# First experts' weights loaded during the first convolution, into a buffer shared with its centred input; ScalarE's copies of x in another order

## What is computed

```
x = x + _L0_conv_ref(_ln_c(x), ...)          # norm over channels, 7x7 depthwise convolution + bias
t = _to_tokens(x)                            # 9216 tokens of 128 channels
t = t + _L0_ffn_ref(_ln_t(t), Wg, W1, W2)    # 8 experts, each token goes to its best 2: silu(x@W1[e])@W2[e]
x = _from_tokens(t, x)
x = x + _L1_conv_ref(_ln_c(x), ...)          # upsample, leaky relu, clip, downsample
t = _to_tokens(x)
t = t + _L1_ffn_ref(_ln_t(t), ...)           # 8 gated experts, best 2
```

## Time and profile before

| | |
|---|---|
| time, median of 3 runs | 1369.09 us (1368.41 to 1370.15) |
| profiled execution, its own time | 1366.47 us |
| profiled execution, span | 1364.7 us |
| TensorE / VectorE / ScalarE / GpSimd busy | 80% / 68% / 47% / 54% of the span |
| first convolution | 0 to 154 us of the span |
| routing before the first block | 156 to 264 us |
| first layer's blocks | from 264 us |

### The profile page before, as it was taken

The page is one execution under the profiler, slowest core; times in us unless marked ns, Lnnn a source line. Parts: engine busy times, 40 slices in busy tenths (PEclk is TensorE's granted clock), DMA queues, the critical chain, the costliest instruction groups (busy, mean ns, idle before and its releaser), DMA issues. The chain is left out here.

```text
span 1364.7 us, 26463 instructions
## 1 busy us (share of the span) xinstructions
PE 1086.2 (80%) x6194; PEld 857.1 (63%) x6194; DVE 930.4 (68%) x3628; ACT 642.2 (47%) x1379; POOL 739.2 (54%) x719
## 2 busy tenths in 40 slices
PE   1499422499999998999389889789879679999982
PEld 0499412388887887989255555455545368888872
DVE  5766344388666675665366767667776588888897
ACT  1456334355555543444434745555654425555441
POOL 0233336567777777654440663663663776666652
PEclk9999855599999998999689989889989779999996
DMA  9243153322222224221610121121110223333498
GB/s 203 84 115 111 31 175 88 81 66 77 75 79 74 76 76 159 84 69 48 188 51 1 48 61 36 38 67 38 29 30 17 63 77 94 92 93 93 115 247 246
DMA packets 100984, 119.24 MB, mean 87 GB/s; under 512 B 29041, under 2 KB 81712, under 8 KB 99950
## 3 DMA queue, kind: packets, MB, share of 16 engines
q1 hardware_dynamic: 68031, 70.36, 20.1%
q0 software_dynamic: 20928, 40.15, 9.9%
q10 hardware_dynamic: 11887, 7.12, 1.9%
HBM read 67.55 MB, written 46.27 MB: 83 GB/s over the span
## 5 line engine op out<-in xcount | busy, mean ns | idle before, releaser
L637 POOL DMA_INDIRECT routed<-r_xn,r_slot x160 | 176.3, 1102 | 201.7 <-DVEq L626 158.7
L1170 POOL DMA_INDIRECT routed<-r_xn,r_slot x160 | 157.9, 987 | 80.4 <-issue 59.2
L1284 POOL DMA_INDIRECT answers<-c_x x152 | 150.8, 992 | 81.0 <-ACT c_x L1277 52.4
L1633 POOL DMA_INDIRECT answers<-c_c x152 | 146.6, 965 | 87.5 <-issue 65.0
L2058 PE MATMUL c_pz<-c_c,down 116*120 116x512 f32 (+1 forms) x392 | 193.3, 609 | 0.0
L1268 PE MATMUL r_ps_xy<-w,c_x 128*128 x1216 | 165.8, 280 | 22.9 <-DVE e_xl L1225 22.3
L1268 PEld LDWEIGHTS r_ps_xy<-w,c_x 128*128 128x128 f32 x1216 | 148.9, 193 | 32.2 <-issue 31.5
L1258 DVE COPY c_x<-r_ps_ht 128x512 f32<-128x512 f32 x152 | 104.3, 686 | 62.9 <-PE r_ps_ht L1250 61.1
L2032 PE MATMUL c_py<-c_xh,gl 121*116 121x512 f32 (+1 forms) x196 | 118.5, 604 | 30.1 <-DVE c_xl L2171 22.3
L1277 ACT ACTIVATE c_x<-r_ps_xy,c_x 128x128 f32<-128x128 f32 x152 | 55.7, 367 | 147.1 <-PE r_ps_xy L1268 145.4
L2181 DVE SCALAR_TENSOR_TENSOR c_c<-c_a 116x1024 f32<-116x1024 f32 (+1 forms) x60 | 76.9, 1281 | 67.6 <-ACT c_a L2119 66.5
(11 more groups left out here) (274 smaller groups left out, 2836.5 us busy)
## 6 DMA issues: line engine op xcount, KB each, us to landing
answers<-answers SPq DMA_DIRECT2D x23, 480.0 KB, 4.4
c_c<-routed SPq DMA_DIRECT2D x159, 66.0 KB
c_w<-in_w SPq DMA_DIRECT2D x26, 393.8 KB, 3.7
c_x<-routed SPq DMA_DIRECT2D x152, 66.0 KB
routed<-r_xn,r_slot POOLq DMA_INDIRECT x320, 2.4
c_x<-in_xh SPq DMA_DIRECT2D x4, 1170.0 KB, 8.5
w1l<-in_w SPq DMA_DIRECT2D x2, 2048.0 KB, 10.3
out<-x ACTq DMA_DIRECT2D x16, 240.0 KB
```

The costliest lines, as they stand in the source:

```text
L637: ro.nc.gpsimd.indirect_dma_start(ro.xs, bass.IndirectOffsetOnAxis(ap=ro.slot[0:px, q, c:c + 1], axis=0), ro.xn[0:px, q, k, t, :], None).t ...
L1170: ro.nc.gpsimd.indirect_dma_start(ro.xs, bass.IndirectOffsetOnAxis(ap=ro.slot[0:px, q, c:c + 1], axis=0), ro.xn[0:px, q, k, t, :], None).t ...
L1284: ex.nc.gpsimd.indirect_dma_start(ex.ys, bass.IndirectOffsetOnAxis(ap=ex.dest[:, slot:slot + 1], axis=0), ex.y[:, slot, :], None).then_inc ...
L1633: ex.nc.gpsimd.indirect_dma_start(ex.ys, bass.IndirectOffsetOnAxis(ap=ex.dest[:, s:s + 1], axis=0), ex.y[:, s, :], None).then_inc(ex.store ...
```

## The change

1. `cen` and the first layer's W1 and W2 now share one buffer (`c0_cen_w`, 26 x 384 floats a partition). For that `cen` is laid out with the channel outermost. Each quarter of it that `centre` writes now steps 384 floats (1536 bytes) from element to element, ScalarE's `square` reads it with the same step, and GpSimd reads a run.
2. The weights are loaded in four halves of 1 MB by SyncE in the convolution's channel loop, after the ring loads 10, 14, 20 and 25, each behind a wait until `normed` tells that the channels in its place have been used. At the end of the phase SyncE waits for all four (`w_loaded`). The two weight DMAs of the second phase are gone, and with them ScalarE's wait for them.
3. The shared buffer's last columns serve as three of the eight landing slots.
4. ScalarE's copies of x after group 4 now come as `COPIED` says: 5, 6 | 7, 8 | 9, 10 | 11 | 12, 13 beside groups 1 to 5, and 14 to 19 one a step in the first six block steps. `first_half` of group 0 comes before normalise of group 1, and the third root of variances one group later. VectorE's measures of groups 7 and 8, and the scale of that batch, come one group later too.

```diff
-        cen = sb("c0_cen", [P, NW, CIN])
+        cen = wt.shared[:].rearrange("p (c n) -> p n c", n=NW)
...
                 sp.dma_start(wring[0:CP, i % WRING, :], io["w0"][i]).then_inc(w_in[i % WRING], 16)
+                if i in WEIGHT_STEPS:
+                    weights_load_half(wt, sp, io, normed, WEIGHT_STEPS.index(i), w_loaded)
             sp.wait_ge(route_consts, 16 * 9)
             sp.wait_ge(blank_in, 16)
+            sp.wait_ge(w_loaded, 16 * len(WEIGHT_STEPS))
...
+WEIGHT_STEPS = (10, 14, 20, CIN - 1)
...
+def weights_load_half(wt, sp, io, normed, n, w_loaded):
+
+    layer_two, half = divmod(n, 2)
+    dst, name = (wt.w2, "w2_0") if layer_two else (wt.w1f, "w1_0")
+    cols = EXPERTS * FF // 2
+    covered = (n + 1) * cols
+    sp.wait_ge(normed, min(-(-covered // NW), CIN))
+    some = slice(half * EXPERTS // 2, (half + 1) * EXPERTS // 2)
+    src = io[name][:, some].rearrange("p e c d -> p (e c d)") if layer_two else io[name][:, some].rearrange("p e f -> p (e f)")
+    sp.dma_start(dst[:, half * cols:(half + 1) * cols], src).then_inc(w_loaded, 16)
...
+        COPIED = (range(0), range(5, 7), range(7, 9), range(9, 11), range(11, 12), range(12, 14), range(14, 14))
...
             for g in MOVED_BY_SP:
                 first_move(ro, sp, c0_x, g)
-                if g == MOVED_BY_SP[3]:
-                    weights_load(wt, sp, io, 0, w_in)
...
             def high_w(e):
-                act.wait_ge(w_in, 32)
...
                 for k in range(3):
-                    if g == (0, 1, 3)[k]:
+                    if g == (0, 1, 4)[k]:
                         first_root(ro, act, k)
+                if g == 1:
+                    first_half(ro, act, 0)
                 first_normalise(ro, act, g)
-                if g:
+                if g > 1:
                     first_half(ro, act, g - 1)
...
-                if 0 < g < BEFORE:
-                    for n in range(3 * g + 2, 3 * g + 5):
-                        first_copy_x(ro, act, n)
+                for n in COPIED[g]:
+                    first_copy_x(ro, act, n)
...
+                if s < GROUPS - COPIED[BEFORE].stop:
+                    first_copy_x(ro, act, COPIED[BEFORE].stop + s)
...
-                if g < 2:
-                    for n in range(BATCHES[2][0] + 2 * g, BATCHES[2][0] + 2 * g + 2):
+                if g in (0, 2):
+                    for n in range(BATCHES[2][0] + g, BATCHES[2][0] + g + 2):
                         first_measure(ro, dve, n)
                         first_spread(ro, dve, n)
-                    if g == 1:
+                    if g == 2:
                         first_variance(ro, dve, 2)
-                elif g == 2:
+                elif g == 3:
                     first_scale(ro, dve, ch, 2)
-                elif g == 3:
                     for n in range(4):
                         table(0, 1 + n)
```

More of the change, by code:

```diff
@@ L148, in after, with conv0_phase @@
         need(self.eng, self.sem, self.base + self.n, beat)
-def conv0_phase(nc, io, r, xs, x):
+def conv0_phase(nc, io, r, xs, x, wt, w_loaded):
     with ExitStack() as ctx:
@@ L386, in __init__, with take_high @@
         self.down = sb("down", [P, N_DOWN * TPX])
+WEIGHT_STEPS = (10, 14, 20, CIN - 1)
+class SharedWeights:
+    def __init__(self, nc, ctx):
+        self.shared = ctx.enter_context(nc.sbuf_tensor("c0_cen_w", [P, NW * CIN], F32))
+        cut = lambda n: self.shared[:, n * EXPERTS * FF:(n + 1) * EXPERTS * FF]
+        self.w1f, self.w2, self.rest = cut(0), cut(1), self.shared[:, 2 * EXPERTS * FF:]
+        self.w1l = self.w1f.bitcast(F32R)
+    def take_high(self, nc, ctx):
+        self.w1h = ctx.enter_context(nc.sbuf_tensor("w1h_0", [P, EXPERTS * FF], F32R))
+def weights_load_half(wt, sp, io, normed, n, w_loaded):
[7 more added lines that the diff above has]
+    sp.dma_start(dst[:, half * cols:(half + 1) * cols], src).then_inc(w_loaded, 16)
 class ExpertWeights:
@@ L932, with __init__ @@
 class FirstRouter:
-    def __init__(self, nc, ctx, sem, r, xs, ps_t, ps_lr, ps_early):
+    def __init__(self, nc, ctx, sem, r, xs, ps_t, ps_lr, ps_early, rest):
         sb = lambda n, s, d=F32: ctx.enter_context(nc.sbuf_tensor(f"r0_{n}", s, d))
@@ L948, in __init__ @@
         self.scattered = [sem(f"scattered{q}") for q in range(QT)]
-        self.landing = sb("landing", [P, LANDING, CGS, IG, CIN])
+        shared = rest.shape[-1] // (CGS * IG * CIN)
+        own, rest = sb("landing", [P, LANDING - shared, CGS, IG, CIN]), rest[:, 0:shared * CGS * IG * CIN].rearrange(
+            "p (s k t c) -> p s k t c", k=CGS, t=IG, c=CIN)
+        self.landing = [own[:, n] for n in range(LANDING - shared)] + [rest[:, n] for n in range(shared)]
         self.x_in = [sem(f"x_in{s}") for s in range(LANDING)]
@@ L985, in first_move @@
     for cg in range(CGS):
-        eng.dma_start(ro.landing[0:pixels(q), slot, cg].rearrange("p t c -> p (t c)"),
+        eng.dma_start(ro.landing[slot][0:pixels(q), cg].rearrange("p t c -> p (t c)"),
                      c0_x[cg * SIDE + ROWS * q:cg * SIDE + ROWS * q + rows, ig * SIDE * IG:(ig + 1) * SIDE * IG, :].rearrange(
@@ L994, in first_copy_x @@
     need(act, ro.x_in[slot], 16 * CGS * (turn + 1))
-    ro.nc.scalar.activation(ro.r.x[0:px, g].rearrange("p t (k c) -> p t k c", c=CIN), ro.landing[0:px, slot].rearrange("p k t c -> p t k c"),
+    ro.nc.scalar.activation(ro.r.x[0:px, g].rearrange("p t (k c) -> p t k c", c=CIN), ro.landing[slot][0:px].rearrange("p k t c -> p t k c"),
                             ACT.Copy).then_inc(ro.x_copied, 1)
@@ L1300, in route0_expert0_phase @@
         ps_xy, ps_h, ps_ht = ([bank(f"{n}{i}") for i in range(2)] for n in ("xy", "h", "ht"))
-        ro = FirstRouter(nc, ctx, sem, r, xs, bank("t"), bank("lr"), ps_xy[0])
+        ro = FirstRouter(nc, ctx, sem, r, xs, bank("t"), bank("lr"), ps_xy[0], wt.rest)
         tb = FirstTables(nc, ctx, sem, r)
@@ L1311, in route0_expert0_phase @@
         fa, fb, down_b = room(N_UP * PPX), room(N_UP * PPX), room(N_DOWN * TPX)
-        w_in, w_high, w_low, tails, factors_in, g_ready, gh_ready = (
-            sem(n) for n in ("w_in", "w_high", "w_low", "tails", "factors_in", "g", "gh"))
+        w_high, w_low, tails, factors_in, g_ready, gh_ready = (
+            sem(n) for n in ("w_high", "w_low", "tails", "factors_in", "g", "gh"))
         block = ctx.enter_context(nc.Block(no_gpsimd_drain=True))
+        COPIED = (range(0), range(5, 7), range(7, 9), range(9, 11), range(11, 12), range(12, 14), range(14, 14))
         PICK = {g: (15 * (g - BEFORE)) // 2 for g in range(BEFORE, GROUPS)}
@@ L2321, in metaformer @@
             x = inner.enter_context(nc.sbuf_tensor("c0_x", [P, NW, CIN], F32))
-            conv0_phase(nc, io, r, xs, x)
-            wt = ExpertWeights(nc, inner, 0)
+            wt = SharedWeights(nc, inner)
+            w_loaded = nc.alloc_semaphore(name="w0_loaded")
+            kept.append(w_loaded)
+            conv0_phase(nc, io, r, xs, x, wt, w_loaded)
+            wt.take_high(nc, inner)
             route0_expert0_phase(nc, io, r, wt, xs, ys, x, kept)
```

## The result

| | before | after |
|---|---|---|
| time, median of 6 runs beside each other | 1368.45 us (1366.82 to 1370.15) | 1358.54 us (1356.66 to 1361.95) |
| ratio, 95% interval | | 0.9927 [0.9915, 0.9939] |
| profiled execution, own time and span | 1366.47 and 1364.7 us | 1360.83 and 1359.0 us |
| first convolution matmul | 55.75 us | 61.91 us |
| first move issued | 156.40 us | 162.96 us |

The change makes the kernel 9.9 us faster, and the interval reaches from 8.3 to 11.6 us. In the trace the first block transpose comes 7.6 us earlier and the last answer of the first layer 7.2.

A forecast was written before the change was run, and what follows sets the result against it. The second stage was taken as waits, bound by SyncE's queue and ScalarE's copies with group 6's routing. Terms -14.3 + 0.3 + 6.5 = -7.5 us took 1369.1 to 1361.6 us; range 1354 to 1368, the forecast's own 1358 to 1365.

The forecast's parts named there:

- Part 1: Second stage: weights leave SyncE's queue, moves end 11.1 us earlier, first block waits for its load, not group 6's logits: -14.3 us.
- Rival (d): Start of the blocks: something else holds queue or routing, only the two weight issues are saved: 1373.0 us, chance 0.07.
- The two chains that end close together: Before the blocks: SyncE's queue plus a landing, and ScalarE's copies plus some 6.8 us of group 6's routing, which ends last.
- Part 2: First six block steps: six ScalarE copies of 0.633 us beside the blocks, mostly hidden: +0.3 us, bounds 0 and 3.8.
- Part 3: Convolution: the weight halves land by 148 us, before its end at 154, and ring loads stay hidden: 0.
- Part 4: Front: stepping layout of `cen` makes `centre` 1.8 us and `square` 1.1 us longer, so everything behind shifts: +6.5 us.
- GpSimd's first scatter: Second stage: held to 195.04 us while 4 MB moved, it can start earlier; 48 scatters done near 252, before the first answer.
- rival e: Start of the blocks: TensorE's clock rises later; 4 us later costs some 2 us; no chance of its own given.

The follow-up runs named there:

- experiment 1: The changed kernel with W1 and W2 loaded again by two 2 MB DMAs behind SyncE's fourth move: 1371.18 us.
- experiment 2: The changed kernel plus one idle 2 MB load of W1 behind SyncE's fourth move: 1366.32 us.
- experiment 5: The kernel before with only the new order of ScalarE's copies, halves and roots and VectorE's measures; weights stay in the second phase: 1364.89 us.
- experiment 6: The changed kernel with ScalarE's and VectorE's old order: 1363.74 us; the same with the shared buffer in pairs of channels: 1358.61 us.
- experiment 4: The kernel before with only the channel-outermost layout of the centred input, in a buffer of its own: 1375.27 us.
- experiment 3: The changed kernel with the shared buffer in pairs of channels, two adjacent floats before each hop: 1352.69 us.

## Why the prediction was right, and where its terms were off

The forecast was 1361.6 us; 1358.5 was measured, within the range and 3.1 us lower, faster as forecast.

- **Part 1, -14.3 us at the stage's start.** The mechanism held. Read from the first move to the first transpose, before took 107.61 us (264.01 - 156.40) and after 93.49 (256.45 - 162.96): -14.1. To the first product it is -13.9. The parts of it: a move costs 1.09 us instead of my 1.04, so the moves' stretch shrank by 10.2 us, not 11.1. The first load followed the last move by 4.54 us (I had 4.3) and the transpose followed it by 1.88 (I had 2.1). The switch from TensorE's order to the queue came as said. That the 9.16 us stall is due to the weight loads, which I held by its place alone, experiments 1 and 2 show: it goes and comes with them, and half of them give half of it. Rival (d) fell with them. The first transpose waits for the load, and group 6's logits end 20.6 us before it: the cover that I put at 17 us or more.
- **The two chains that end close together.** The weights alone would have given 9.5 us in the median, and the order alone 4.2; both together, with the layout's price taken out by pairs, 15.8 (1368.51 to 1352.69). In the trace the order's share of the stage is 3.1 us if it comes first (experiment 5) and 3.7 or 4.9 if it comes second (experiment 6), because each uncovers the other. The prediction had this mechanism, and no number for each part.
- **Part 2, +0.3 us.** From the first transpose to the last answer took 387.15 us before and 387.51 after, and 387.93 in the second profile of after. No single wait shows it; it is of the size taken, and within the scatter.
- **Part 3, 0.** The last megabyte is issued at 140.38 us and landed 5.8 us later, before the convolution's end; a ring load's median went from 3.7 to 4.1 us, and from the first matmul to the phase's first move the change takes 101.05 us, as long as experiment 4 (101.12), where no weights move in the convolution. Held.
- **Part 4, +6.5 us.** Measured +6.2 in the first matmul, +6.56 in the first move, +6.2 (alone) and +5.9 (undone) in medians. The sum hit, and its terms erred against each other: `centre` cost 1.63 us more (I took 1.8), `square` 2.00 (I took 1.1, half of the nearest surcharge, with a doubling as its bound; it was the doubling). I had the last squares' sum at 50.1 and it stands at 50.19. (My 50.1 holds a term that the working doesn't list: the second, smaller piece of `square`, L222, 0.38 us in the kernel before. Without it 46.4 + 2.14 + 1.1 is 49.6.) Per element the write's step cost 1628/2496 = 0.65 ns, where my three quarters of the surcharge of two stepping streams gave 0.73. The table of the Trainium skill that the prediction cites (Vector Engine (DVE) Microarchitecture Reference, "Measured stream behaviour on trn2") has 1.71 less 1.05 ns, 0.66, for a hop of 4 KiB, and was the better estimate.
- **GpSimd's first scatter** (a side remark): I held that the 4 MB kept it, and a part of the wait is theirs. What the scatter needs last are the slots that VectorE writes. With weights under way in the second phase (before, experiments 1, 2, 4 and 5) it starts 6.2 to 6.8 us behind these, without them (the change, experiments 3 and 6) 3.6 to 4.4. So some 2 us were the weights', and the rest I can't explain. The page's idle time before it fell from 12.25 to 7.33 us. It gained nothing, since the scatters were through by 259.4, ahead of the first answer at 264.41.
- **The clock (rival e).** It rose to full 7.1 us behind the first transpose before, and 4.7 us after, instead of later as I feared:

```profile
257.00:261.00 4.00, 3.19 (x9) 2.48 (x10) 1.19 (x8) 0.63 (x2) 1.99 (x2) 0.50 0.45 111
261.10:265.10 4.00, 3.78 (x27) 3.05 (x26) 3.75 (x28) 1.95 (x4) 0.05 (x1) 1.00 0.29 70
```

These are windows of after (columns as in the earlier trace rows), the granted clock is 0.50 (1.2 GHz) in the first and 1.00 (2.4 GHz) in the second; in before shows 0.50 up to 271, and from 271.1 to 275.1 it is 1.00. The earlier rise is worth some 0.6 us at the first answer (8.53 us behind the first transpose before, 7.96 after), and most of it is not there any more at the last one.

What stays open are 2.4 us: the sum of the terms was -7.5, the last answer in the trace came 7.2 us earlier (6.4 between the two second profiles), and the medians differ by 9.9. The profiled executions lie 2.0 and 1.6 us below the median of before and 2.3 and 3.7 above that of after, while others lie from 2.8 below to 5.6 above, and most of that scatter arises in the untouched third phase. The stage times of one kernel agree to some tenths from profile to profile (107.61 and 107.72, 93.49 and 93.52), though kernels that should agree can differ by 1 to 2 us (experiment 4's 105.77 beside before). So I trust them for the mechanism, and leave the rest of the median unexplained.

## What to carry to other kernels

A DMA queue that issued many small transfers paid here for a large one twice, for its issue and for the stall while its bytes were under way (2.8 and 8.2 us in the kernel before); move such a transfer to a stretch in which nobody waits for the queue, even if it takes a shared buffer. Before pricing such a move look for the second chain that ends close behind: here two edits were worth 9.5 and 4.2 us alone, and one uncovered the other. And where a layout makes an element-wise write or read hop, keep two neighbouring words together: the same sharing of the buffer cost 5.9 us with single words and nothing with pairs.

## What the runs showed of the hardware

- ScalarE's read that steps 1536 bytes from element to element took 4.14 us for 2304 elements instead of 2.14 (1.80 against 0.93 ns each), a larger surcharge than VectorE's write with the same step (0.65 ns). In pairs it took 2.23, 4% more than in order.
- A move's issue behind 4 MB took 9.1 to 9.8 us and behind 2 MB 4.42, and in each case it was one single issue, some 4 to 5 us behind the start of the last large one's own.
- GpSimd's multiply of 384 elements took 1.31 us with steps of 104 bytes, 1.10 in order and 1.12 with steps of 8 bytes: a gain of 16%. It reaches nobody, since TensorE waits for VectorE's low parts:

```profile
L206 POOL TENSOR_TENSOR c_nrm<-c_cen_w,c_rstd 120x384 f32<-120x384 f32 x26 | 28.4, 1098 | 114.8 <-DVE c_pl L325 58.9
```

- GpSimd's first scatter of the phase started 4.25 us behind the slots that it needed last (193.04 to 197.29 us) in the change, and 6.47 in the kernel before, with 4 MB under way.
